# Second mixture of experts: bias addition moved to the PSUM copies, first weighted rows to ScalarE

## The reference, cut to what matters

```python
combine, dispatch = top2_dispatch(xf, Wg, C)            # per group, C = 22
def moe_apply(x, combine, dispatch, W, b):
    disp = jnp.einsum('sec,sd->ecd', dispatch, x)
    h = jnp.einsum('ecd,edf->ecf', disp, W) + b[:, None, :]
    return jnp.einsum('sec,ecf->sf', combine, h)
h = moe_apply(xf, combine, dispatch, W1, b1)            # 128 -> 512
h = jax.nn.relu(layer_norm(h, ln_hid_w, ln_hid_b))
out = moe_apply(h, combine, dispatch, W2, b2)           # 512 -> 128
return layer_norm(out + x, ln_out_w, ln_out_b)
```

## Time and profile before

| | us |
|---|---|
| median of 3 runs | 430.27 |
| lowest, highest | 425.24, 430.97 |
| profiled execution | 429.6 |
| its span, first to last instruction | 427.9 |
| TensorE busy | 381.2 (89%) |
| VectorE busy | 263.7 (62%) |
| ScalarE busy | 192.8 (45%) |
| GpSimd busy | 117.2 (27%) |

### The profile page before, as it was taken

One profiled execution on the slowest core, in us unless ns is written; L12 is line 12 of the kernel. 1 busy time (PEld: TensorE's weight loads), 2 busy tenths in 40 slices (PEclk: granted clock), 3 DMA queues, 4 the chain that ended last, 5 costly groups with the idle time before them and its releaser, 6 DMA issues.

```text
span 427.9 us, 7077 instructions
## 1 busy us (share of the span) xinstructions
PE 381.2 (89%) x2675; PEld 216.7 (51%) x2675; DVE 263.7 (62%) x682; ACT 192.8 (45%) x303; POOL 117.2 (27%) x160
## 2 busy tenths in 40 slices
PE   8998968999897999999998899987997897999961
PEld 3675447874343232333332585644575332788951
DVE  4777703325788789889823886626168637893435
ACT  5323102310506567776787596655625541533200
POOL 4013785460507146100110000110000055744042
PEclk9995997999999799999999999996899998999976
DMA  4499514014167444000000000005999487322132
GB/s 116 134 141 330 210 44 115 30 44 113 37 185 191 106 121 103 3 1 3 2 3 0 2 1 2 0 0 204 389 294 290 159 264 227 121 79 63 41 81 55
DMA packets 35877, 46.03 MB, mean 108 GB/s; under 512 B 4778, under 2 KB 21682, under 8 KB 35844
## 3 DMA queue, kind: packets, MB, share of 16 engines
q1 hardware_dynamic: 33156, 38.57, 32.0%
q0 software_dynamic: 2688, 7.02, 5.9%
HBM read 31.67 MB, written 13.78 MB: 106 GB/s over the span
## 4 chain that ended last, share of the span: by engine, by line
PE 58%; DVE 12%; issue 8%; DMA 6%; ACT 6%; POOL 4%; another core or an unknown queue 4%; POOLq 0%; SPq 0%; DVEq 0%; ACTq 0%
PE ps L1438 7%; PE ps L1694 7%; PE ps L1680 7%; PE ps L1655 6%; PE ps L1990 4%; PE ps L1663 3%; PE ps L2015 2%; PE ps L1943 2%; PE ps L1852 2%; PE ps L1799 2%; POOL y_d L593 2%; PE ps L1442 2%; PE ps L1808 2%; PE ps L1599 2%
## 5 line engine op out<-in xcount | busy, mean ns | idle before, releaser
L1255 DVE TENSOR_REDUCE early<-ps 128x1 f32<-128x512 f32 x128 | 81.6, 685 | 13.2 <-PE ps L1655 9.8
L812 ACT ACTIVATE R<-ps 128x1024 f32<-128x1024 f32 x64 | 62.6, 1019 | 23.9 <-PE ps L1680 23.0
L1680 PE MATMUL ps<-R 75*128 75x512 bf16 x128 | 38.8, 391 | 2.2 <-DMA R<-R 2.1
L1655 PE MATMUL ps<-R 72*128 72x512 bf16 x112 | 39.2, 392 | 0.8 <-DVE early L1255 0.8
L1438 PEld LDWEIGHTS ps<-ident,R 128*77 128x77 f32 (+1 forms) x216 | 24.2, 145 | 23.1 <-issue 9.9
L663 POOL DMA_INDIRECT R<-h_d,srow x16 | 15.4, 963 | 73.8 <-DMA h_d<-ff 67.6
L1438 PE MATMUL ps<-ident,R 128*77 128x128 f32 (+1 forms) x216 | 31.7, 280 | 4.2 <-ACT R L804 1.8
L1694 PE MATMUL ps<-R,vaug 128*9 128x512 f32 x256 | 34.3, 609 | 0.6 <-ACT R L812 0.6
L1442 PE MATMUL ps<-early,ones_b 128*128 128x512 bf16 (+1 forms) x119 | 30.6, 403 | 1.6 <-POOL ident L532 1.6
L1655 PEld LDWEIGHTS ps<-R 72*128 72x128 bf16 x112 | 11.0, 98 | 32.5 <-DVE early L1255 19.6
L1221 DVE TENSOR_SCALAR R<-ps,vcol 128x256 f32<-128x256 f32 x16 | 7.0, 479 | 25.2 <-remote 13.4
(11 more groups left out here) (340 smaller groups left out, 717.6 us busy)
## 6 DMA issues: line engine op xcount, KB each, us to landing
R<-in_L_ffn_W_dram SPq DMA_DIRECT2D x1, 6144.0 KB, 19.7
h_d<-R SPq DMA_DIRECT2D x12, 256.0 KB, 4.7
q_d<-R SPq DMA_DIRECT2D x24, 96.0 KB, 1.9
R<-k_d SPq DMA_DIRECT2D x24, 96.0 KB
R<-q_d SPq DMA_DIRECT2D x8, 288.0 KB
R<-in_L_ffn_w_dram SPq DMA_DIRECT2D x1, 2048.0 KB
h_d<-ff SPq DMA_DIRECT2D x6, 256.0 KB, 4.6
disp_d<-R SPq DMA_DIRECT2D x1, 1032.0 KB, 13.0
```

The costliest lines, as they stand in the source:

```text
L812: s.activation(probs[idx % 4], ps[:, 2 * (idx % 2):2 * (idx % 2) + 2, :].rearrange("p b t -> p (b t)"), ACT.Exp, scale=QK_SCALE).then_inc( ...
L1255: v.tensor_reduce(mcol[:, u, col:col + 1], bank(ring_bank("row", n)), AX.X, ALU.max).then_inc(s1_max, 1)
L1655: m.matmul(bank(ring_bank("row", n)), Q9[0:KQ, b, h, t * P:(t + 1) * P], K9[0:KQ, b, h, :], start=True, stop=True).then_inc(s1_mm, 1)
L1680: ins = m.matmul(bank(2 * (idx % 2) + j), K9[0:KM, b, h, kt * P:(kt + 1) * P], Q9[0:KM, b, h, :], start=True, stop=True)
```

## The change

b1 and b2 are laid out in SBUF once per slot: six loads of [128, 512] (b1rep) and six of [128, 128] (b2rep), each expert's row repeated on 32 partitions, issued by SP between W1 and W2 after the last projection of cross attention. VectorE copies quads 0 to 11 with the bias added; for quads 12 to 17 TensorE adds the bias by a bf16 product of three stacked parts of b1 (`b1_parts`, split on GpSimd at unit 3 of self attention) with a 0/1 matrix (`of_slot`, made by ScalarE), and ScalarE copies them. The transposes of comb, `hidden_bias` and `output_bias` are gone. All blocks of the second product are copied by VectorE with b2 added. ScalarE makes gate times row 0 for pairs 1 to 7 in PSUM; the epsilon of the variance becomes the square root's bias. VectorE's comb comes after the copies, the LNW, LNB and t1 operations after the pair loop; the last part of pair 1 is made by VectorE, the twelve transposes of `early` go before hidden_group(0); out_order is (0, 3, 1, 2).

```diff
-        out_order = (0, 1, 3, 2)
+        out_order = (0, 3, 1, 2)
...
+            for part in range(3):
+                sp.dma_start(bstage[32 * part:32 * part + E1, :], a["L1_ffn_b1"]).then_inc(ld_hid, 16)
+                sp.dma_start(bstage[32 * part + E1:32 * part + 32, :], a["L1_ffn_b1"][0:32 - E1, :]).then_inc(ld_hid, 16)
...
             sp.dma_start(W1, a["L1_ffn_W1"].rearrange("e m h -> m e h")).then_inc(ld_W1, 16)
+            sp.wait_ge(proj_mm, 2 * B)
+            for quad in range(QUADS):
+                sp.dma_start(b1rep[quad], a["L1_ffn_b1"][4 * quad:4 * quad + 4, :].unsqueeze(1).to_broadcast([4, 32, F1])).then_inc(ld_rep, 16)
+            for quad in range(QUADS):
+                sp.dma_start(b2rep[:, D * quad:D * (quad + 1)],
+                             a["L1_ffn_b2"][4 * quad:4 * quad + 4, :].unsqueeze(1).to_broadcast([4, 32, D])).then_inc(ld_rep, 16)
             sp.dma_start(W2, a["L1_ffn_W2"].rearrange("e (k f) m -> f (e k) m", f=P)).then_inc(ld_W2, 16)
-
-            sp.wait_ge(logits_mm, 2)
-            sp.dma_start(b1_1, a["L1_ffn_b1"]).then_inc(ld_hid, 16)
-            sp.dma_start(b2_1, a["L1_ffn_b2"]).then_inc(ld_hid, 16)
...
-                if q == 3:
+                if q == 2:
                     last_rest(0)
-                    last_rest(1)
...
-                s.activation(tmp8[:, q:q + 1], tmp8b[:, q:q + 1], ACT.Sqrt).then_inc(hstd, 1)
+                s.activation(tmp8[:, q:q + 1], mv[:, q, 1:2], ACT.Sqrt, bias=eps6[:, :]).then_inc(hstd, 1)
+
+            def inner_part(q):
+                t = paired[q]
+                act.wait_ge(gathered[t], 32)
+                if q == 1:
+                    act.wait_ge(gates_ready, 1)
+                if q >= 2:
+                    act.wait_ge(hvar, q - 1)
+                s.activation(bank(PART_BANK[q % 2]), got1[q % 4][:, 0, :], ACT.Copy, scale=gate[1][:, 0, t:t + 1]).then_inc(hpart, 1)
...
             evac_slots1(1)
-            for i in range(QUADS):
-                copy_quad(i)
+            act.wait_ge(proj_mm, 2 * B)
+            for part in range(3):
+                rows = slice(32 * part, 32 * part + 32)
+                ins = s.copy(of_slot[rows, :].rearrange("p (e c) -> p e c", c=32),
+                             ident[rows, 32 * part:32 * part + E1].unsqueeze(2).to_broadcast([32, E1, 32]))
+            ins.then_inc(of_slot_ready, 1)
             evac_slots1(2)
...
+            evac_slots1(3)
             def copy_last(i):
                 act.wait_ge(w_tp, B + i + 1)
                 s.copy(lastT_flat[:, 512 * i:512 * (i + 1)], bank(LAST_BANK[i])).then_inc(wT_ready, 1)
...
-            copy_quad(7)
-            copy_quads(9, 11)
-            evac_slots1(3)
-            copy_quads(12, 13)
+            copy_quad(12)
+            copy_quad(13)
+            inner_part(1)
             hid_std(0)
-            copy_quads(14, 16)
+            copy_quad(14)
+            copy_quad(15)
+            copy_quad(16)
             hid_std(1)
             copy_quad(17)
+            copy_last(0)
+            inner_part(2)
+            evac_hidden(0)
             hid_std(2)
-            for c in range(4):
-                evac_hidden(c)
+            inner_part(3)
+            evac_hidden(1)
+            evac_hidden(2)
             hid_std(3)
-            for i in range(3):
-                copy_last(i)
+            evac_hidden(3)
+            copy_last(1)
+            copy_last(2)
+            inner_part(4)
+            evac_hidden(4)
             hid_std(4)
-            for c in range(4, 7):
-                evac_hidden(c)
+            inner_part(5)
+            evac_hidden(5)
+            evac_hidden(6)
             hid_std(5)
             evac_hidden(7)
+            inner_part(6)
             hid_std(6)
-            copy_block(0, 0)
-            copy_block(0, 1)
+            inner_part(7)
             hid_std(7)
             for c in range(8, 15):
                 evac_hidden(c)
...
+            def copy_quads(first, last):
+
+                dve.wait_ge(ld_rep, 16 * 2 * QUADS)
+                for i in range(first, last):
+                    blk, slot = i // QUADS, i % QUADS
+                    dve.wait_ge(h1_mm, i + 1)
+                    if blk >= 1:
+                        wait_half_stored(dve, blk - 1, slot // 3)
+                    v.tensor_tensor(ring[slot], bank(W1_BANKS[i % 3]), b1rep[slot], ALU.add).then_inc(h1_dve, 1)
...
+                    copy_quads(0, QUADS)
...
+                    copy_quads(QUADS, 2 * QUADS)
...
+            for q in range(T):
+                t = paired[q]
+                inner, rest = hsum[q % 6], hrest[q % 6]
+                partial = bank(PART_BANK[q % 2])
+                if q == 0:
+                    dve.wait_ge(gathered[t], 32)
+                    me.link(v.tensor_scalar(partial, got1[0][:, 0, :], g1[:, 0, t:t + 1], None, ALU.mult))
+                else:
+                    dve.wait_ge(hpart, q)
+                if q >= 6:
+                    dve.wait_ge(hdisp_mm, 4 * ((q - 6) // 2 + 1))
+                me.link(v.scalar_tensor_tensor(out=inner, in0=got1[q % 4][:, 1, :], scalar=g1[:, 1, t:t + 1],
+                                               in1=partial, op0=ALU.mult, op1=ALU.add))
+                me.link(v.bn_stats(st6[:, q, :], inner))
+                v.bn_aggr(mv[:, q, :], st6[:, q, :]).then_inc(hvar, 1)
+                dve.wait_ge(hstd, q + 1)
+                me.link(v.reciprocal(rstd[:, q:q + 1], tmp8[:, q:q + 1]))
+                me.link(v.tensor_scalar(inner, inner, mv[:, q, 0:1], rstd[:, q:q + 1], ALU.subtract, ALU.mult))
+                v.tensor_tensor(rest, inner, top(inner), ALU.subtract).then_inc(hid_r1, 1)
+                if q == 1:
+                    dve.wait_ge(hid_r1, 2)
+                    v.tensor_tensor(hlast[1], rest, top(rest), ALU.subtract).then_inc(hid_p3, 1)
             lnw = bias[:, R_LNW, :]
             me.step(v.tensor_scalar(lnw, lnw, tg[:, 3:4], None, ALU.mult))
             me.link(v.tensor_scalar(bias[:, R_LNB, :], bias[:, R_LNB, :], tg[:, 3:4], None, ALU.mult))
             me.step(v.tensor_tensor(t1[:, :, :], t3[:, :, :], bias[:, R_LNB:R_LNB + 1, :].to_broadcast([P, T, D]), ALU.add))
...
-            add_bias_rows()
+
+            def copy_block(blk):
+                for part in range(2):
+                    dve.wait_ge(y1_mm, 2 * blk + part + 1)
+                    for half in range(2):
+                        wait_half_stored(dve, BLOCKS - 1, half)
+                    columns = (4, 2)[part] * D
+                    v.tensor_tensor(yblock[blk][part], ps[:, BLOCK_BANK[blk] + part, 0:columns],
+                                    b2rep[:, 4 * D * part:4 * D * part + columns], ALU.add).then_inc(y1_dve, 1)
+
+            copy_block(0)
...
+                if i == 1:
+                    copy_block(1)
+                    copy_block(2)
...
+            def quad_bias(i):
+                wait_quad_copied(pe, i - 3)
+                m.matmul(bank(W1_BANKS[i % 3]), of_slot[:, P * (i % QUADS):P * (i % QUADS + 1)], b1_parts, start=True, stop=False)
...
-            pe.wait_ge(comb_ready, 1)
-            for t in range(T):
-                ins = tp(ps[0:E1, 4 + t // TB, (t % TB) * P:(t % TB + 1) * P], comb[:, t, :], P)
-                if t % TB == TB - 1:
-                    ins.then_inc(comb_tp, 1)
             first_product(1, 0)
             first_product(1, 1)
             dispatch(3)
-            pe.wait_ge(ld_hid, 32)
-            hidden_bias(0)
-            first_product(2, 0)
-            hidden_bias(1)
-            first_product(2, 1)
-            hidden_bias(2)
-            hidden_bias(3)
-            for i in range(BLOCKS * QUADS - 3, BLOCKS * QUADS):
+            pe.wait_ge(bias_parts, 1)
+            pe.wait_ge(of_slot_ready, 1)
+            last = BLOCKS * QUADS
+            for i in range(last - QUADS, last - QUADS + 3):
+                quad_bias(i)
+            pe.wait_ge(slots1T_ready, NG)
+            for i in range(last - QUADS, last):
+                if last - QUADS + 2 <= i < last - 1:
+                    quad_bias(i + 1)
+                quad_products(i, False)
+            for b in range(B):
+                pe.wait_ge(w_ready, 3 + b)
+                for i in range(QUADS):
+                    at = QUADS * b + i
+                    ins = tp(ps[:, LAST_BANK[at // 4], at % 4 * P:(at % 4 + 1) * P], early[b][:, P * i:P * (i + 1)], P)
+                    if at % 4 == 3:
+                        ins.then_inc(w_tp, 1)
+            for i in range(last - 3, last):
...
-            hidden_bias(6)
-            hidden_bias(7)
...
-            output_bias(0)
-            output_bias(1)
```

More of the change, by code:

```diff
@@ L49 @@
 BLOCKS = 3
-DVE_QUADS = (6, 8)
+DVE_QUADS = tuple(range(12))
 W1_BANKS = (2, 3, 1)
@@ L243, in flamingo_kernel @@
         hlast = [v[:, F1:HP].bitcast(BF16) for v in hpieces]
-        b1_1 = xT[0:E1, 0:F1]
-        b2_1 = xT[0:E1, F1:F1 + D]
+        b1rep = [v[:, F1 * i:F1 * (i + 1)] for v in (
```

(25 more changed lines are left out.)

108 lines of the change are left out of this document (28 added, 80 removed).

## The result

The changed kernel took 442.79 us (median of 4 runs, 439.91 to 452.32), the kernel before, beside it on the same chip, 430.62 (4 runs): 1.0303 of before, with a 95% interval of 1.0153 to 1.0454. The forecast was 425.3, with a range of 419 to 431.5. The change costs 3% by the middle of this interval, and the time lies outside the range. The profiled execution took 444.52, with a span of 442.8.

A forecast was written before the change was run, and what follows sets the result against it. The prediction took a relay between engines, then TensorE alone from 371.52 us, then a relay again as the bound. Its terms -1.5 - 1.9 - 4.0 + 2.4 = -5.0 took 430.27 to 425.3 us, range 419 to 431.5.

The forecast's parts named there:

- Part 1: Front up to group 1's dispatch (371.5 us): VectorE's bias copies, load order, pair loop; -1.5 us, bounds -2.7 and +2.0.
- rival 3: First products: the backlog of W2 leaves all 6.7 us of the bias loads uncovered; 432.0 us, chance 0.05.
- The cover is used up, not exceeded.: VectorE's copies of quads 9 to 11, waiting for block 0's stores, end at 348.1 to 349.3, against 349.2 before.
- The pair loop: VectorE's loop loses the first weighted row and the epsilon: 4.34 us a pair becomes 3.4.
- Part 2: TensorE from group 1's dispatch: bias rows leave the chain, -3.9 us; waits they hid return, +2.0; net -1.9.
- Part 3, the hole: Before 412.5 us, TensorE's second products come in bunches after GpSimd's first gather of block 1's rows; change avoids this, -4.0 us.
- Part 4, the tail: From block 2's copy to the end: VectorE's serial chain, group 1 now behind the weighted sum; +2.4 us.
- D: Theory from the experiments, not the prediction: block 1's late copy delays GpSimd's last eight gathers and lengthens the tail, 2 to 3 us.

The follow-up runs named there:

- no_loads: The changed kernel without its twelve loads of repeated biases and the wait for them, so those biases are missing: 417.63 us, 0.9861 of before.
- staged: The changed kernel with each bias first repeated in DRAM during self attention and loaded from there with 128 source rows: 421.04 us, 1.0032 of before.
- before_loads: The kernel before with only the six loads of b1rep added between W1 and W2, waited for but not used: 435.26 us, 1.0301 of before.
- staged_order: staged with output order 0, 1, 3, 2 instead of 0, 3, 1, 2: 428.38 us, 1.0055 of before.
- staged_order_b: staged_order measured again in the fifth set, on one chip beside other versions: 424.89 us, 0.996 of before.
- copy1_first: staged_order with VectorE copying block 1 ahead of output group 0 instead of behind it: 428.96 us, 0.9934 of before.
- copy1_first_b: copy1_first measured again in the fifth set, on one chip beside other versions: 421.13 us, 0.9875 of before.
- by_expert: The changed kernel with each b1rep load cut into four of one expert (one row repeated 32 times), b2rep loaded from DRAM copies: 429.91 us, 1.0112 of before.
- w2_first: The changed kernel with W2 issued ahead of the twelve loads of repeated biases: 446.99 us (one run), 1.036 of before.
- tensor_bias: The changed kernel with all eighteen quads' bias by bf16 product, no b1rep, b2rep from DRAM copies behind W2, order 0, 1, 3, 2: 430.79 us, 1.0146 of before.

## Why the prediction was wrong

**The step that failed** stands in Part 1: "SP now issues 1.57 + 0.39 MB of repeated biases between W1 and W2 ... 1.96 MB at 291 GB/s are 6.7 us: W2 ends near 340.4, with the stores of block 0, from 335 on, beside it." Two errors are in it. The price was bytes by the rate of another load, W2, which filled all engines (share 1.06). The loads ran at 97 to 99 GB/s and held SP from 294.5 to 328.1; W2 landed at 354.1 (issue at 328.69 plus 25.4), not 340.4. And the stores were put beside W2, where they stand behind it: the first issue, at 332.62, holds SP until 350.61. The sentence on the Trainium skill right behind had the second point (a store can't pass W2) and left it to rival 3 at 5%, because no row of before showed a store behind W2. That was the row to build: what stands behind the 6 MB, and since when. In place of 0 to +6.7 us the step cost +20 (56.5 measured against 36.6 in no_loads): 3.5 of them are there with full engines too (40.1 in staged), the other 16.4 come from the four rows.

**"The cover is used up, not exceeded."** Even with the loads at full rate it is exceeded, by about half of the 6.7: staged needs 40.1 us for that stage, no_loads 36.6, before 38.6.

**The rest of Part 1, -1.5.** Right in size once the loads are away: 38.6 became 36.6 in no_loads. The pair loop: two second weighted rows without a wait between them in the trace of after start 3.46 apart (376.70 and 380.16), where I had 3.4 and before 4.34. Pair 4's square root was late, as I said for others of them: VectorE waits 2.62 for hid_std(4) behind evac_hidden(4).

```profile
388.83 0.16 DVE L1419 RECIPROCAL rstds<-tmp 128x1 f32<-128x1 f32 x1 [2.62 <-ACT tmp L925]
```

**Part 2, -1.9.** -1.1 in after and -1.4 in no_loads and staged (23.17 against 24.57): right in sign, and of the 3.9 that went more than the 2.0 forecast came back.

**Part 3, the hole, -4.0.** Wrong in its reason. The bunches are no fixture of either kernel: before_loads, whose TensorE program is that of before, ran its 336 products in one piece, and so did staged; after has them, only at the other end, ahead of the 330:

```profile
404.73 9.38 PE L2022 MATMUL ps<-R 128*32 128x128 f32 x336
...
413.50 0.43 PE L2057 MATMUL ps<-R 128*32 128x128 f32 x4 [0.44 <-issue]
414.92 9.33 PE L2057 MATMUL ps<-R 128*32 128x128 f32 x330 [0.99 <-issue]
```

The first line is before_loads, the others after. The stage is 16.4 us in before and 14.5 in after, but 11.9 in before_loads and in no_loads alike: without bunches it is the same with and without the change, which gains nothing here. staged_order and staged_order_b are one program, as are copy1_first and copy1_first_b; each time the first has bunches (in earlier products) and the second has none. So they are a matter of the single execution. The prediction had seen that (the lowest run lay 5 us below the median) and still took the whole 4.0 as the change's. What makes the bunches I don't know: in after they come during GpSimd's gathers of block 0's rows, but staged has such gathers and no bunches.

**Part 4, the tail, +2.4.** +3.6 in after. The serial chain is as worked out: group 3 2.87 us (429.77 to 432.64), the last two groups behind it without a wait, 3.95 each. Group 1 behind the weighted sum is the loss, as the forecast had it. What was missed is the start: from the copy of block 2 to group 3 went 5.9 us, not 0.7 + 2.7, though the weighted sum ran at full clock. Its records end at 427.54, 2.2 us ahead of group 3. In no_loads and staged nothing lies between, and the same step takes 3.7: so the 2.2 belong to single executions, like the bunches. In those two traces the gathers make up for it: VectorE waits 3.3 and 2.2 us for rows behind group 3. I had worked out VectorE's chain alone and left GpSimd out, whose eight gathers of 1.25 us follow one another once block 1 is copied late; the copies' move to VectorE puts them there. This is also why the old order alone gave nothing in two sets: group 1, put back ahead of group 3, waits for its rows. The early copy gained 0.9 to 1.2%, if D holds. Whether the new order still costs something behind an early copy stays open (0.9994 against 0.9934).

**The rivals.** Rival 3 named the right queue, with 6.7 us; its mechanism came true at three times the price, and the reason for that price, the four rows, is in no rival. Its chance of 5% rested on "the copies need block 0's stores only from 343 on", which no longer helps once W2 starts 36 us late.

## What to carry to other kernels

A load's price is its bytes over the engines that it gets, and in these runs it got them by the outer dimension of its source: repeating a few rows over all partitions is the case to look at, since the tile is 128 wide and the source is not. Repeat the rows in DRAM early, or give every repeat its own outer rows. Before putting anything ahead of a large transfer, list what stands behind that transfer in the same queue and who needs it: here the victims were neither the loads nor W2 but six stores of 256 KB. And take a gap in one profiled execution for the change's only when a second execution of the same program has it.

## What the runs showed of the hardware

- A load of 256 KB with four source rows held SP's queue 2.7 us; with 128 rows 0.64 to 0.83 (staged), with 32 rows and 64 KB 0.42 (0.46 from issue to issue, by_expert). The DMA share was 0.26 to 0.30 from 312 to 330 in after; in staged and by_expert it stayed above 1.0 from 296 to 326.
- Behind 6 MB of W2, one issue held SP for 27.88 us (before_loads), 28.56 with its pair (w2_first) and 28.16 (tensor_bias), though the loads themselves were small. It was let go a little before W2 had landed: 329.30 against 333.75 in before, 350.61 against 354.1 in after.
- A full share is not one rate: W1 moved at 385 to 399 GB/s at a share of 1.05 (after, 300 to 310), W2 at 290 at the same share (342 to 346). Their contiguous pieces are 2 KB and 512 bytes; that this is the reason is not shown.
- The records of TensorE and the start of the engine that waits for it can lie apart: the last second product of before ends at 411.26, its copy begins at 412.53; the weighted sum ends at 427.54 in after, group 3 begins at 429.77, where in staged it is 400.39 and 400.43. What TensorE does in between the traces do not show.
